# A decoder layer on one core: VectorE's loop cut at another place of the same order

## The reference, cut to what matters

```python
def _L0_attn_ref(x, ...):            # 16 heads of 32
    q, k, v = heads(x @ Wq + bq), heads(x @ Wk + bk), heads(x @ Wv + bv)
    scores = einsum(q / |q|, k / |k|) / (sigmoid(x.mean(axis=1) @ Wt + bt) + 0.5)
    vals, idx = jax.lax.top_k(scores, 64)          # a quarter of 256 keys
    out = (softmax(vals) scattered to its keys) @ v @ Wo + bo
    gate = jax.nn.sigmoid(x @ Wg + bg)
    return gate * out + (1.0 - gate) * x
x = _layernorm(x + _L0_attn_ref(x, ...))
x = _layernorm(x + _L0_xattn_ref(x, ctx_512, ctx_512, ...))    # one head, softmax
x = _layernorm(x + _L0_ffn_ref(x, W, b, ids, weights))         # sum of 8 adapters
```

## Time and profile before

| | us |
|---|---|
| median of 3 runs | 3202.72 |
| lowest, highest | 3202.55, 3206.73 |
| the profiled execution | 3211.29 |
| its span, first to last instruction | 3209.3 |
| TensorE, VectorE, ScalarE, GpSimd busy in it | 2837.4, 2729.7, 2119.9, 1583.2 |
| mean granted clock of TensorE, share of full speed | 0.959 |

### The profile page before, as it was taken

One profiled execution on the slowest core, in us unless ns is written; L12 is line 12 of the kernel. 1 busy time (PEld: TensorE's weight loads), 2 busy tenths in 40 slices (PEclk: granted clock), 3 DMA queues, 4 the chain that ended last, 5 costly groups with the idle time before them and its releaser, 6 DMA issues. The chain is left out here.

```text
span 3209.3 us, 58791 instructions
## 1 busy us (share of the span) xinstructions
PE 2837.4 (88%) x16154; PEld 1560.3 (49%) x16154; DVE 2729.7 (85%) x10113; ACT 2119.9 (66%) x5970; POOL 1583.2 (49%) x2285
## 2 busy tenths in 40 slices
PE   6799999989899789998998999999988998989755
PEld 4455555545455345554554555555545554545333
DVE  4889889888888898888888898988988898888881
ACT  3577777766576557766766777777767776657541
POOL 3345555545455444554544554555545454545422
PEclk8899999999999989999999999999999999999877
DMA  6000000000000000000000000000000000000000
GB/s 226 8 18 25 25 24 22 19 10 24 24 25 22 5 24 25 25 22 4 25 25 24 25 21 25 17 13 25 25 24 22 24 18 11 24 24 18 9 10 13
DMA packets 43674, 80.04 MB, mean 25 GB/s; under 512 B 3914, under 2 KB 12106, under 8 KB 43186
## 3 DMA queue, kind: packets, MB, share of 16 engines
q1 hardware_dynamic: 41682, 69.18, 6.6%
q0 software_dynamic: 1504, 5.77, 0.5%
HBM read 58.16 MB, written 16.78 MB: 23 GB/s over the span
## 5 line engine op out<-in xcount | busy, mean ns | idle before, releaser
L523 POOL TENSOR_SCALAR probs<-probs,kept_inv 128x256 f32<-128x256 f32 x1024 | 474.0, 486 | 611.0 <-DVE kept_inv L1905 611.0
L789 ACT ACTIVATE scores<-score_ps,neg_guess 128x256 f32<-128x256 f32 x1024 | 397.5, 480 | 233.4 <-DVE kept_inv L1905 197.8
L1867 DVE SCALAR_TENSOR_TENSOR probs<-scores,threshold,probs 128x256 f32<-128x256 f32 x1011 | 434.0, 492 | 137.5 <-ACT unsure_n L815 107.5
L809 ACT ACTIVATE near<-scores 128x256 f32<-128x256 f32 x1024 | 411.3, 415 | 4.2 <-DVE nearest L1834 1.1
L824 ACT ACTIVATE probsT<-work_ps 128x512 f32<-128x512 f32 x512 | 292.7, 597 | 181.0 <-PE work_ps L1122 178.4
L1830 DVE MATCH_REPLACE8 near<-nearest,near 128x256 f32<-128x256 f32 x1024 | 406.8, 407 | 0.0
L1122 PE MATMUL work_ps<-ident,probs 128*128 128x128 f32 x2072 | 324.0, 291 | 79.2 <-POOL probs L523 36.7
L1826 DVE MAX8 nearest<-near 128x8 f32<-128x256 f32 x1024 | 358.1, 410 | 9.8 <-DVE near L1818 8.7
L1834 DVE MAX8 nearest<-near 128x8 f32<-128x256 f32 x1024 | 356.9, 409 | 0.0
L490 POOL TENSOR_TENSOR inv_norm<-sumsq,minus_half 128x32 f32<-128x32 f32 x64 | 351.2, 5488 | 5.3
L1818 DVE TENSOR_SCALAR near<-scores,flip 128x256 int32<-128x256 int32 x1024 | 307.1, 367 | 4.5
(11 more groups left out here) (173 smaller groups left out, 5484.0 us busy)
## 6 DMA issues: line engine op xcount, KB each, us to landing
x_in<-in_x_dram SPq DMA_DIRECT2D x32, 512.0 KB, 3.7
x_res<-in_x_dram SPq DMA_DIRECT2D x32, 512.0 KB, 3.6
out_dram<-rows SPq DMA_DIRECT2D x32, 512.0 KB, 3.0
c_sb<-in_ctx_dram SPq DMA_DIRECT2D x32, 256.0 KB, 2.7
rows<-in_L_ffn_W_dram SPq DMA_DIRECT2D x8, 512.0 KB, 4.7
gate_t<-in_L_ffn_W_dram SPq DMA_DIRECT2D x3, 512.0 KB, 3.7
v_sb<-in_L_ffn_W_dram SPq DMA_DIRECT2D x3, 512.0 KB, 4.5
w_q<-in_L_attn_Wq_dram POOLq DMA_DIRECT2D x1, 1024.0 KB, 8.9
```

The source lines that it names most:

```text
L523: pool.tensor_scalar(probs[:, s % 2, h, j], probs[:, s % 2, h, j], kept_inv[:, s % 2, n:n + 1], 1.0, ALU.mult, ALU.mult).then_inc(s_pr, 1)
L789: last = act.activation(scores[:, s % 2, h, j], score_ps[:, j, h], ACT.Identity, bias=neg_guess[:, t, n:n + 1])
L809: last = act.activation(near[:, h, j], scores[:, s % 2, h, j], ACT.Sign, accum_out=sign_sum[:, s % 2, n:n + 1])
L1867: step.mark(dve.scalar_tensor_tensor(out=probs[:, r, h, j], in0=scores[:, r, h, j], scalar=threshold[:, r, k:k + 1], in1=probs[:, r, h, j] ...
```

## The change

VectorE's loop is cut at another place of the same endless order: a body now begins with set_threshold(i,0) and mixing(i-1), and ends with search(i+1,0,1). The same is done to TensorE's body for attend(2) and the turns of unit 3, whose list is written out, so that the order of its instructions stays. In ScalarE's setup two pairs of copies change places.

```diff
@@ ScalarE, setup @@
             take_queries(0, 0)
-            keep_cross_weights(8, 1)
             keys_to_16(0, 1)
             queries_to_16(0, 0)
+            keep_cross_weights(8, 1)
             take_key_moments(0)
             take_queries(0, 1)
+            queries_to_16(0, 1)
             keep_cross_weights(9, 2)
-            queries_to_16(0, 1)
             take_key_sums(0)
@@ TensorE, body(i, p, where) @@
+                if behind:
+                    pe.wait_ge(s_pt, at(i - 1, 16, 10))
+                    attend(i - 1, 2, 1 - p)
+                    pe.wait_ge(s_pt, at(i - 1, 16, 12))
+                    turn_probs(i - 1, 3, 0, 0)
...
+                    turn_probs(i - 1, 3, 1, 1)
                 if ahead:
...
                 if here:
                     pe.wait_ge(s_fl, at(i, 4, 4))
                     out_project(i, 0)
-                    pe.wait_ge(s_pt, at(i, 16, 10))
-                    attend(i, 2, p)
-                    pe.wait_ge(s_pt, at(i, 16, 12))
-                    turn_probs(i, 3, 0, 0)
...
-                    turn_probs(i, 3, 1, 1)
@@ VectorE, body(i, p, where) @@
                 step.restart()
+                if here:
+                    set_threshold(i, 0)
+                if behind:
+                    mixing(i - 1, 1 - p)
                 if ahead:
                     if where != "fill":
                         query_sums(i + 1, 0)
...
                     search(i + 1, 0, 0)
                     search(i + 1, 0, 1)
-                    set_threshold(i + 1, 0)
-                if here:
-                    mixing(i, p)
```

More of the change, by code:

```diff
@@ L1365, in body @@
                 behind = where in ("second", "steady", "last", "drain")
+                if behind:
[3 more added lines that the diff above has]
+                    turn_probs(i - 1, 3, 0, 0)
+                    if where == "drain":
+                        pe.wait_ge(s_pt, at(i - 1, 16, 9))
+                    else:
+                        pe.wait_ge(s_v, at(i, 2, 2))
+                    turn_probs(i - 1, 3, 0, 1)
+                    pe.wait_ge(s_at, at(i - 1, 4, 3))
+                    turn_probs(i - 1, 3, 1, 0)
+                    pe.wait_ge(s_pt, at(i - 1, 16, 13))
+                    turn_probs(i - 1, 3, 1, 1)
                 if ahead:
```

## The result

The changed kernel takes 3233.77 us (median of 3 runs, 3227.15 to 3234.83) against 3202.72 before: a ratio of 1.0083, 95% interval 1.0067 to 1.0098. It is slower, as forecast, but by 31 us instead of 8.7, and the time lies above the range. The profiled execution has a span of 3225.2 us where before had 3209.3.

What follows compares the result with a forecast made beforehand. Clean items were taken as bound by the round through TensorE, with VectorE in it at a few points. Per jump 2.05 - 0.80 = 1.25, less 0.58, is 0.67 us; times 13, +8.7 us: median 3211.4 us, range 3202 to 3225.

Steps and rivals of the forecast that it cites:

- What of the fetch shows: VectorE, at each jump: the threshold behind the four MAX8 starts 2.05 us late (ends 1.9 and 3.02).
- the end of 3.02: VectorE, at each jump: upper end of the visible fetch, the whole idle time, if nothing overlaps with MAX8.
- The collision: VectorE's L1847 after each jump no longer meets GpSimd's subtraction L545: gain 0.80 us (ends 0 and 0.80).
- All 1.25 us go to TensorE's idle time at turn_x1: Mixing late by 1.25 us at each jump makes TensorE idle that long, mostly at turn_x1.
- 0.58 us given back: Behind mixing, the jump's old place: the 0.58 us each jump costs the item there is regained.
- The setup, and TensorE's order: ScalarE's exchanged setup copies and TensorE's unrolled block: cost 0; at most 0.6 us once if a setup cover were missing.
- In iterations without a jump the clear has taken no visible time so far, and it goes under the four MAX8 of the search: 0.: VectorE's clear, moved from behind mixing to behind the search, costs 0 in items without a jump.
- The clock: TensorE: a new idle stretch might drop its clock, 1.7 us more a jump; chance 0.04, not in the sum.
- the clock rival: TensorE's clock drops in the new idle stretches: +22 us on top of the forecast, 3233; chance 0.04.

Runs made afterwards that it cites:

- setup_only: The kernel before with only ScalarE's two pairs of copies in the setup exchanged: 3207.86 us, ratio 1.0004.
- after_clear_kept: The changed kernel with one more wait-and-clear between mixing and query_sums, where the kernel before has it: 3220.70 us, ratio 1.0044.
- after_no_overlap: The changed kernel with VectorE's sequencer held before the jump until the four MAX8 are done (a wait and an increment added): 3258.61 us, ratio 1.0157.
- the second: The changed kernel, unedited, measured again with a trace of its own against the kernel before: 3230.26 us, ratio 1.0074.

## Why the prediction was right in sign and wrong in size

The sum of after against `setup_only`, steady stretch, 22.8 us measured:

| cause | predicted | by the runs |
|---|---|---|
| 13 jumps, each the late mixing less what the old place gave back | 13 x (1.25 - 0.58) = 8.7 | 13 x 0.57 = 7.4 |
| the clear no longer behind mixing | 0 | 28 x 0.29 = 8.1 |
| short half-speed stretches of TensorE | 0 (chance 0.04) | 5 x 1.3 = 6.5 |
| sum | 8.7 | 22.0 |

The 0.57 is an item with and one without a jump in `after_clear_kept`, 91.75 + 90.48, less the same two over before and `setup_only`, 91.10 + 90.56. The 0.29 is after's two, 92.04 + 90.78, less those of `after_clear_kept`, 91.75 + 90.48 (0.29 and 0.30). Both are carried over from the 18 short items to the ten long ones, where single differences between traces reach 2 us; that the sum meets 22.8 doesn't prove the shares to the us. Taken from whole steady stretches, with 1.3 us for each fall, the clear's share is 9.0 + 1.3 = 10.3 us (after less `after_clear_kept`) and that of the jumps 13.8 - 7.8 = 6.0 (`after_clear_kept` less `setup_only`).

- **What of the fetch shows**: right. 2.05 us was taken, 25.6 / 13 = 1.97 measured, by the same row-of-four-MAX8 argument. `after_no_overlap` shows what it would be without: more than the end of 3.02, because it waits longer before the jump and the jump is longer too.
- **The collision**: right. L1848 takes 0.29 us behind the jump. From L1842's start to the end of the statistics 6.03 us pass instead of 6.70: 0.67 of the 0.80 us.
- **All 1.25 us go to TensorE's idle time at turn_x1**: right. In `after_clear_kept`, where this is the only change but for the clock, the item with a jump is 91.75 - 90.48 = 1.27 us longer than the one without.
- **0.58 us given back**: right to about 0.1 us, though not only because VectorE is earlier: while the jump stood there it also kept norm1 at 3.47 us. **The setup, and TensorE's order**: right, both nothing.
- **"In iterations without a jump the clear has taken no visible time so far, and it goes under the four MAX8 of the search: 0."**: this step failed, for 8 to 10 us. The clear took no time of VectorE that the waits show, and from this I concluded that it did nothing. It held VectorE's next operations back by 0.09 us while norm1 ran beside them, and norm1 lies on the path that bounds the item. I had looked at what the moved instructions cost, not at what they held apart. The same row that I used for the jump's collision (L1847, 1.09 us against 0.29) should have made me ask about every other pair of VectorE and GpSimd operations at the place left behind.
- **The clock**: this step failed too, for 6.5 to 7.8 us. It was given 0.04, at 1.7 us in each of 13 jumps, and nothing in the sum; it came in 5 or 6 of them at 1.3 us. The prediction leaned on a single row, 1.08 us of idling at turn_x1 with the clock at 1.00. In `after_clear_kept`, where the pause is the forecast one (1.11 to 1.39 us at turn_x1's first tile, 0.53 at its second), the clock fell at 6 of 13 places, and the 1.08 us of the earlier trace rows too had 0.53 us behind them. The size of the pause was forecast rightly; that one place kept its clock said little about 13 others. That 3233 us was the time of the clock rival and nearly the time measured is a coincidence: of the 14 us by which the 22.8 exceed the forecast 8.7, the clock has under half.

The median moved by 31.0 us in the first comparison and by 23.9 in the second, with overlapping intervals (1.0067 to 1.0098, 1.0061 to 1.0088); the sum above explains the traces' 22.8. The profiled execution of after was the fastest of its three (3227.15 us, mean granted clock 0.960); the other two, 3234.83 and 3233.77, have 0.957 and 0.956. That points to more time at half clock in them, but no trace of them shows it, so the 7 us between them and the profiled one stay open.

## What to carry to other kernels

The cut of a rolled loop costs what of the fetch isn't covered by operations already queued, plus what the next engine on the bounding path then waits: put it behind a long row of queued operations and far from a hand-over to that path. An instruction, or an idle time, that costs nothing may still be holding two engines' operations apart, so when something is moved, look at who runs beside whom at the place it leaves, by the lengths of the same operation in two places: before's own trace had norm1 at 4.24 and at 3.47 us. And when a pause opens on TensorE, one like pause that left the clock alone is weak evidence: here such pauses lowered it at 5 or 6 of 13 places.

## What the runs showed of the hardware

- **What VectorE does beside GpSimd's normalisation sets its length**: five operations take 3.47 us while VectorE idles, 4.24 with VectorE's next operation behind the clear, 4.51 with it 0.09 us earlier, and 4.09 or 4.41 with it 0.13 us later. An operation on 32-bit data can stretch while the other engine works: L1847 takes 1.09 us beside the subtraction L545 and 0.29 alone, while L545, which had begun first, takes 1.27 us both times; the pair at L538 takes 2.29, 2.16 and 1.52 us. The Trainium skill ("SBUF — State Buffer", Who interferes with whom) has VectorE operations with two SBUF inputs and GpSimd operations that read SBUF exclude each other, the first to start going first. L1847 (two inputs) beside L545 agrees; which pairs meet in norm1 operation by operation was not worked out.
- **Useless instructions made a kernel faster**: an added wait-and-clear by 9.6 us (1.0074 to 1.0044, intervals apart), two semaphore increments in every item from 1.0074 to 1.0050 and two rows of useless turns on TensorE per pair of items to 1.0055. For the last two the intervals overlap, and the steady stretch is shorter by 9.5 and 6.5 us.
- **The clock falls to half behind pauses of 1.19 to 1.70 us and 0.53 us** at 5 or 6 of 13 like places, largely the same from execution to execution, 1.3 us lost each time. Filling the longer pause removes all of the falls. Why those places and not the others is open.
- **The jump's fetch isn't of one length**: 2.8 us from branch to next instruction in after, 3.9 us in `after_no_overlap`, whose loop differs from it by two instructions.
